# A graph layer's first stage: a third buffer for finished rows and a fifth for the input

## The chip, the cores and the metric

The kernel runs on one core of a Trainium2 chip. The time is that of one launch on the device in microseconds. Three runs gave 759.32, 760.2 and 762.78 us, so the median is 760.2 us. A fourth run was profiled.

## The reference

6250 nodes with 256 features each pass through one layer of a graph network, all in fp32:

```python
xn = layernorm(x)
x = x + gnn(xn, edge_index, weight, attn_l, attn_r) + mix(xn, w_qkv, w_out, b_out)
x = x + moe(layernorm(x), router and expert weights)
```

`gnn` needs two tables per node: `xt = xn @ weight` (256 columns) and the attention scores `xt . attn_l` and `xt . attn_r` of four heads each. For node n it takes the left score of row `src[n]`, the right score and the features of row `dst[n]`, makes a softmax over the four heads and sums the heads with it. `mix` is linear attention: keys and values are products of xn with 512 columns each, normalised per head over 64 columns, and `k^T v` is summed over all nodes. `moe` sends each node to two of six experts of three layers.

## The kernel before, in words

The nodes are laid out as 125 partitions by 50 tiles, `x_t = x.rearrange("(p t) n -> p t n")`. Ten chunks of CH = 5 tiles (CHUNKS) are the unit of transfer. Two tiles make a pair; there are PR = 25 pairs.

**First stage** (what the change touches). For each tile it makes the layer norm xn, its transpose in two parts x_h and x_l (together the exact fp32 value), which stay in SBUF, and the row of both tables, which goes to HBM, since the gathers of the next stage read it there. The engines work on it like this:

- SP (the queue engine) issues all transfers in the order in which its program has them, and a wait or a slow issue holds everything behind it. At the start come chunk 0 in two parts, the graph weights `w_g`, the two attention vectors, chunks 1 to 3, `w_kv` (1 MB into `kv_raw`), then seven small ones. After that, for c = 0 to 9: if chunk c + 4 exists, wait until chunk c is normalised and load chunk c + 4 into the buffer it leaves (XB = 4 buffers `xc`); wait until the rows of chunk c are finished and store them, in three transfers: two for the wide table `xt_tab` (112 and 13 partitions) and one for the score table `al_tab` (125 partitions, 4 floats a row). Behind the loop come the second weights `w_q` and `w_oT`, then the expert weights that the next stage converts (`take`, `put`).
- DVE (VectorE) makes the statistics (L826, L830) of two tiles in each step i, 10 tiles ahead of the products; `finish(c)` (L838, L840) makes a chunk's reciprocal `rs` and `nmr` once ScalarE has taken the root; `lower(i)` (L845) makes x_l of pair i. In steps 12 and 14 it also makes the column means of half of `w_kv` (`centre`, L877, L878). The list STATS_AT says in which step the last statistics of a chunk are made; ScalarE's root follows in that step and `finish` at the start of the next.
- POOL normalises (L519) into a ring of four tiles, and between tiles 29 and 37 subtracts the column means from `w_kv` in four parts (`kv_centre`, L536); between tiles 41 and 48 it makes the lower part of `w_kv` (`kv_lower`, L527). Behind the tiles it waits for all stores and then issues the gathers.
- PE (TensorE) transposes pair i + 1 (L1192) and multiplies pair i by the graph weights (L1198, L1199, L1201) in turn; four PSUM banks hold the results.
- ACT (ScalarE) copies the transposes to x_h (`upper`, L640), the table rows out of PSUM into the ring `xts` (`table`, L647; two chunks long, so that chunk c waits for the store of chunk c - 2), takes the roots (`stdev`, L635) and in steps 17 and 19 casts `w_kv` to its upper part (L667).

**Second stage.** Once the last table row is copied and `w_kv` is ready, PE computes keys and values of each tile and sums `k^T v` (dots, L1221). DVE and ACT normalise them, DVE makes the gathered graph sums (from L923), and at step 2 sets `dotsT` to zero (L979), which lies behind `w_q` and `w_oT` in the space `weight_in` and waits for their load. POOL gathers. The later stages (mixed rows and router, experts) are not touched.

All sizes are fixed by hand: `prep` counts VectorE's linked small steps, and PREP_BO and PREP_W are its values at two points.

## Time and profile before

| what | value |
|---|---|
| median of 3 runs | 760.2 us |
| profiled execution | 756.72 us |
| its span in the profile | 754.7 us |
| mean granted clock of TensorE | 0.945 |
| busy: TensorE, weight loads | 89%, 82% |
| busy: DVE, ACT, POOL | 74%, 58%, 59% |
| moved | 104.68 MB, 139 GB/s |

The span is what the hardware profiler saw from the first instruction to the last, and the execution's own time is 2.0 us longer. The granted clock is the share of 2.4 GHz that TensorE was given: 1.00 is 2.4 GHz and 0.5 is 1.2 GHz. "Idle before" an instruction is the time its engine stood still, with what released it last. A busy share is an average over stages with different limits; only the stage in question tells what a change in it is worth. The page's table of 40 slices has about 19 us in each, so that the first stage is the first four.

### The profile page before, as it was taken

The page shows a single profiled execution, that of the slowest core. Times are in us where ns is not written, and L with a number is a line of the kernel's source. Part 1 is how long each engine was busy: PE and PEld are TensorE (multiplying, and loading weights), DVE is VectorE, ACT ScalarE, POOL GpSimd, SP SyncE. Part 2 cuts the span into 40 slices and gives each one's busy share as a digit, 9 for nine tenths or more (in the row PEclk, how much of TensorE's full clock was granted, in tenths as well). Part 3 has the DMA queues.
Part 4 walks back from the last instruction along what each step waited for, and adds up shares of the span by engine and source line. Part 5 has one row for each costly group of instructions (what it writes and reads, how often), then busy time and mean ns, then how long its engine had stood idle before and what let it go on. Part 6 is the DMA issues. An engine that isn't in the chain of part 4 may idle for free.

```text
span 754.7 us, 15722 instructions
## 1 busy us (share of the span) xinstructions
PE 673.2 (89%) x4705; PEld 621.3 (82%) x4705; DVE 555.3 (74%) x1423; ACT 441.1 (58%) x878; POOL 448.4 (59%) x392
## 2 busy tenths in 40 slices
PE   3878999999999979889885099999999999999993
PEld 2868888888888868777764089999999999999993
DVE  5665569998888876877786357777777777777773
ACT  2546567667776636767763145665665665656651
POOL 3547388877666500325556468888888865455555
PEclk9989999999999999988995579999999999999997
DMA  8785644444444268588734478666546965654443
GB/s 223 164 191 139 162 129 127 125 127 122 128 131 129 62 211 290 170 256 249 222 99 139 130 211 191 122 126 121 113 84 100 173 114 95 98 88 58 50 44 37
DMA packets 90673, 104.68 MB, mean 139 GB/s; under 512 B 27196, under 2 KB 74746, under 8 KB 90594
## 3 DMA queue, kind: packets, MB, share of 16 engines
q1 hardware_dynamic: 58049, 70.98, 33.4%
q0 software_dynamic: 32544, 32.70, 25.0%
q8 instruction: 43, 0.70, 0.4%
q14 instruction: 37, 0.30, 0.1%
HBM read 53.25 MB, written 52.26 MB: 140 GB/s over the span
## 4 chain that ended last, share of the span: by engine, by line
PE 77%; DVE 10%; DMA 3%; ACT 3%; POOL 2%; issue 2%; SPq 1%; POOLq 0%; DVEq 0%; ACTq 0%
PE kv_ps L1357 10%; PE kv_ps L1358 10%; PE kv_ps L1359 10%; PE pt L1349 6%; PE d_ps L1221 6%; PE kv_ps L1198 5%; PE kv_ps L1201 5%; PE kv_ps L1199 5%; PE xt_ps L1349 3%; PE kv_ps L1298 2%; PE pt L1201 2%; PE pt L1198 2%; PE pt L1199 2%; POOL tab L588 1%; PE pt L1289 1%
## 5 line engine op out<-in xcount | busy, mean ns | idle before, releaser
L1357 PE MATMUL kv_ps<-we_h,now_h 128*128 x648 | 193.6, 299 | 3.7 <-DVE now_l L1168 2.2
L1358 PE MATMUL kv_ps<-we_l,now_h 128*128 x648 | 184.4, 285 | 0.0
L1359 PE MATMUL kv_ps<-we_h,now_l 128*128 x648 | 184.3, 284 | 0.0
L1357 PEld LDWEIGHTS kv_ps<-we_h,now_h 128*128 128x128 f32 x648 | 125.1, 193 | 5.2 <-issue 5.2
L1358 PEld LDWEIGHTS kv_ps<-we_l,now_h 128*128 128x128 f32 x648 | 125.4, 194 | 0.0
L1359 PEld LDWEIGHTS kv_ps<-we_h,now_l 128*128 128x128 f32 x648 | 124.9, 193 | 0.0
L1148 DVE TENSOR_TENSOR work<-kv_ps,be 128x256 f32<-128x256 f32 x216 | 81.7, 420 | 52.8 <-PE kv_ps L1359 52.6
L610 POOL DMA_INDIRECT out_x<-work,arena x56 | 87.6, 1564 | 41.9 <-DVE work L1156 26.0
L788 ACT ACTIVATE now_h<-pt 128x512 fp32r<-128x512 f32 x54 | 32.5, 602 | 105.9 <-PE pt L1349 105.9
L556 POOL DMA_INDIRECT alg<-al_tab,src_all x50 | 62.3, 1245 | 39.2 <-issue 25.2
L960 DVE TENSOR_REDUCE ss<-xring 125x16 f32<-125x1040 f32 x50 | 61.7, 1234 | 16.9 <-ACT xring L673 15.9
L559 POOL DMA_INDIRECT arena<-xt_tab,dst_all x50 | 62.0, 1240 | 15.2 <-issue 15.2
L1221 PEld LDWEIGHTS d_ps<-work 125*128 125x128 f32 x400 | 52.0, 191 | 4.8 <-DVE work L974 0.9
L1168 DVE TENSOR_TENSOR now_l<-pt,now_h 128x512 fp32r<-128x512 f32 x54 | 37.4, 692 | 23.5 <-ACT now_h L788 23.5
L588 POOL DMA_INDIRECT tab<-work,pos x14 | 16.8, 1198 | 63.2 <-DVE work L1093 59.5
L773 ACT ACTIVATE staged<-arena 128x256 f32<-128x256 f32 x80 | 43.5, 597 | 18.3 <-DMA arena<-tab 18.3
L1221 PE MATMUL d_ps<-work 125*128 125x128 f32 x400 | 52.5, 275 | 0.7 <-DVE work L974 0.7
L599 POOL DMA_INDIRECT tab<-arena x40 | 40.3, 1007 | 20.4 <-issue 10.9
L1198 PE MATMUL kv_ps<-wkv_h,x_h 128*128 128x512 f32 x120 | 49.7, 414 | 0.6 <-ACT arena L647 0.6
L1349 PE MATMUL pt<-ident,staged 128*128 128x128 f32 x216 | 33.3, 278 | 16.6 <-ACT staged L773 16.6
L588 POOL DMA_INDIRECT tab<-arena,pos x24 | 28.7, 1195 | 32.2 <-DVE arena L1093 25.8
L1199 PE MATMUL kv_ps<-wkv_l,x_h 128*128 128x512 f32 x120 | 47.0, 392 | 0.0
(249 smaller groups left out, 1836.1 us busy)
## 6 DMA issues: line engine op xcount, KB each, us to landing
arena<-tab SPq DMA_DIRECT2D x80, 131.0 KB, 2.9
xring<-in_x SPq DMA_DIRECT2D x26, 224.0 KB
xt_tab<-arena SPq DMA_DIRECT2D x10, 568.8 KB
we_h<-wt_h SPq DMA_DIRECT2D x6, 768.0 KB, 6.0
we_l<-wt_l SPq DMA_DIRECT2D x6, 768.0 KB, 8.8
weight_in<-tab SPq DMA_DIRECT2D x28, 131.0 KB, 2.6
xring<-in_x SPq DMA_DIRECT2D x5, 560.0 KB
out_x<-arena SPq DMA_DIRECT2D x12, 224.0 KB
```

Of the source, the lines that this page charges most:

```text
L556: pool.indirect_dma_start(out=alg[:, b, t % CH, :], out_offset=None, in_=al_tab, in_offset=bass.IndirectOffsetOnAxis(ap=src_all[:, t:t + 1 ...
L559: pool.indirect_dma_start(out=xtg[:, b, t % CH, :], out_offset=None, in_=xt_tab, in_offset=bass.IndirectOffsetOnAxis(ap=dst_all[:, t:t + 1 ...
L610: pool.indirect_dma_start(out=out, out_offset=bass.IndirectOffsetOnAxis(ap=rb[u][:, h, C_TOK:C_TOK + 1].bitcast(I32), axis=0), in_=yw[n % ...
L960: dve.reduce_sum(ss[:, t % 2, :], sq[t % 2], axis=AX.X).then_inc(red_done, 1)
L1148: dve.tensor_tensor(rows[:, h, :], outp[:, h, :], be[layer][:, bass.ds(es[n, h] * F, F)], ALU.add).then_inc(finished, 1)
L1198: pe.matmul(outp, x_h[:, t, c, :], w_h(c), start=c == 0, stop=False)
L1199: pe.matmul(outp, x_h[:, t, c, :], w_l(c), start=False, stop=False)
L1221: last = pe.matmul(d_ps[:, at], vs[t % VB][:, at], ks[t % VB][:, at], start=False, stop=t == T - 1, skip_group_check=True)
L1349: last = pe.transpose(outp[:, h, c, :], rows[:, h, c * 128:(c + 1) * 128], ident[:, :])
L1357: pe.matmul(outp, hi[:, c, :], we_h[:, w], start=c == 0, stop=False)
L1358: pe.matmul(outp, hi[:, c, :], we_l[:, w], start=False, stop=False)
L1359: last = pe.matmul(outp, lo[:, c, :], we_h[:, w], start=False, stop=c == KC - 1)
```

## The change

The ring of finished rows gets a third buffer (XS = 3), placed in `weight_in`, and the input a fifth (XB = 5), placed in `work`. Chunk c then waits for the store of chunk c - 3, and chunk c + 5 is loaded when chunk c is normalised. As the third row buffer lies over part of the space of `w_q` and `w_oT`, their load moves behind the first two expert loads and waits for the last store from that buffer. The column means are made in four pieces, in steps 11 to 14, and POOL waits for one piece only. ScalarE takes a root of one column at the very start, whose result is not used. The whole diff:

```diff
--- before.py
+++ after.py
@@ -23,7 +23,7 @@
 KC = D // 128
 CH = 5
 CHUNKS = T // CH
-XB = 4
+XB, XS = 5, 3
 PR = T // 2
 KB, VB, LAG = 4, 3, 3
 XTW = D + GH
@@ -62,7 +62,7 @@
 ROUTE_STEPS = (0, 1, 9, 15)
 ROUTE = {end - 1: g for g, end in enumerate(ENDS)}
 STATS_AT = {c: max(0, -(-(CH * c - 7) // 2)) for c in range(2, CHUNKS)}
-PREP_EPS, PREP_BO, PREP_W = 1, 13, 18
+PREP_EPS, PREP_BO, PREP_W = 1, 15, 20
 POOL_C = 17
 
 
@@ -129,10 +129,11 @@
 
 
         mix_h, mix_l = wg_h[:, :, 0:D], wg_l[:, :, 0:D]
-        xc = [rows[0:P, b * CH * D:(b + 1) * CH * D].rearrange("p (g n) -> p g n", g=CH)
-              for rows in (xring, gsum_sb) for b in range(2)]
+        xc = [rows[0:P, at:at + CH * D].rearrange("p (g n) -> p g n", g=CH)
+              for rows, at in ((xring, 0), (xring, CH * D), (gsum_sb, 0), (gsum_sb, CH * D), (work, 3 * MI))]
         xn = staged[0:P, 0:4 * D].rearrange("p (g n) -> p g n", g=4)
-        xts = arena[0:P, 0:2 * CH * GW].rearrange("p (g n) -> p g n", g=2 * CH)
+        xts = [rows[0:P, at:at + CH * GW].rearrange("p (g n) -> p g n", g=CH)
+               for rows, at in ((arena, 0), (arena, CH * GW), (weight_in, KC * GW + 3 * D))]
         kv_raw = arena[:, 2 * CH * GW:2 * CH * GW + KC * 2 * MI].rearrange("p (c n) -> p c n", c=KC)
         wg_raw = weight_in[:, 0:KC * GW].rearrange("p (c n) -> p c n", c=KC)
         att_bc = weight_in[:, KC * GW:KC * GW + 2 * D].rearrange("p (s n) -> p s n", s=2)
@@ -142,6 +143,7 @@
         st = sb("st", [P, 2 * CH, 6])
         mv = sb("mv", [P, 2 * CH, 2])
         sd = sb("sd", [P, 2 * CH])
+        first_root = sb("first_root", [128, 1])
         rs = sb("rs", [P, 2 * CH])
         nmr = sb("nmr", [P, 2 * CH])
 
@@ -265,7 +267,7 @@
         mean_done, kv_c, kv_hd, kv_ld = sem("mean_done"), sem("kv_c"), sem("kv_hd"), sem("kv_ld")
         bs_done, ag_done, sd_done, fin_done = sem("bs_done"), sem("ag_done"), sem("sd_done"), sem("fin_done")
         xn_ready, pt_ready, xh_ready, xl_ready = sem("xn_ready"), sem("pt_ready"), sem("xh_ready"), sem("xl_ready")
-        xt_ready, xts_done, xt_out = sem("xt_ready"), sem("xts_done"), [sem(f"xt_out{h}") for h in range(2)]
+        xt_ready, xts_done, xt_out = sem("xt_ready"), sem("xts_done"), [sem(f"xt_out{h}") for h in range(XS)]
 
         k_ready, v_ready, sq_eps = sem("k_ready"), sem("v_ready"), sem("sq_eps")
         sqv_done, red_done, vs_ready, pr_done, sr_done = (sem("sqv_done"), sem("red_done"), sem("vs_ready"),
@@ -409,21 +411,21 @@
                     sp.wait_ge(xn_ready, (c + 1) * CH)
                     load_x(c + XB)
                 sp.wait_ge(xts_done, (c + 1) * CH)
-                rows = slice((c % 2) * CH, (c % 2 + 1) * CH)
                 at = slice(c * CH, (c + 1) * CH)
-                wide(xt_t[:, at, :], xts[:, rows, 0:XTW], xt_out[c % 2])
-                sp.dma_start(al_t[:, at, :], xts[:, rows, XTW:GW]).then_inc(xt_out[c % 2], 16)
-
-
-            sp.wait_ge(wg_ld, 1)
-            sp.wait_ge(prep, PREP_BO)
-            sp.dma_start(wq_sb, chunks(w_q)).then_inc(w3_in, 16)
-            sp.dma_start(woT_sb, chunks(w_oT)).then_inc(w3_in, 16)
+                wide(xt_t[:, at, :], xts[c % XS][:, :, 0:XTW], xt_out[c % XS])
+                sp.dma_start(al_t[:, at, :], xts[c % XS][:, :, XTW:GW]).then_inc(xt_out[c % XS], 16)
+
 
             sp.wait_ge(pt_ready, T)
             take(0)
             sp.wait_ge(kv_ld, 4)
             take(1)
+            sp.wait_ge(wg_ld, 1)
+            sp.wait_ge(prep, PREP_BO)
+            sp.wait_ge(xt_out[2], STORE * len(range(2, CHUNKS, XS)))
+            sp.dma_start(wq_sb, chunks(w_q)).then_inc(w3_in, 16)
+            sp.dma_start(woT_sb, chunks(w_oT)).then_inc(w3_in, 16)
+
             for r in range(ROUNDS):
                 sp.wait_ge(cvl_done, r + 1)
                 put(r)
@@ -532,7 +534,7 @@
                 half, c = part // 2, part % 2
                 cols = slice(half * MI, half * MI + MI)
                 kv_v = kv_raw[:, c, cols].rearrange("p (h n) -> p h n", n=MC)
-                pool.wait_ge(mean_done, half + 1)
+                pool.wait_ge(mean_done, part + 1)
                 pool.tensor_tensor(kv_v, kv_v, kv_mean[:, c, half * MH:half * MH + MH].unsqueeze(2).to_broadcast([128, MH, MC]),
                                    ALU.add).then_inc(kv_c, 1)
 
@@ -545,8 +547,8 @@
             pool.wait_ge(xn_ready, T)
             pool.memset(xring[0:P, 0:4 * MH * SQ].rearrange("p (h n) -> p h n", n=SQ)[:, :, MC:SQ], MC * EPS).then_inc(sq_eps, 1)
 
-            for h in range(2):
-                pool.wait_ge(xt_out[h], STORE * (CHUNKS // 2))
+            for h in range(XS):
+                pool.wait_ge(xt_out[h], STORE * len(range(h, CHUNKS, XS)))
             pool.wait_ge(w2_in, W2)
 
             for t in range(T):
@@ -642,11 +644,13 @@
             def table(t):
 
                 act.wait_ge(xt_ready, t + 1)
-                if t % CH == 0 and t >= 2 * CH:
-                    act.wait_ge(xt_out[t // CH % 2], STORE * (t // CH // 2))
-                act.activation(xts[:, t % (2 * CH), :], banks[t % 4][0:P, 0:GW], ACT.Copy).then_inc(xts_done, 1)
+                c = t // CH
+                if t % CH == 0 and c >= XS:
+                    act.wait_ge(xt_out[c % XS], STORE * (c // XS))
+                act.activation(xts[c % XS][:, t % CH, :], banks[t % 4][0:P, 0:GW], ACT.Copy).then_inc(xts_done, 1)
 
             act.wait_ge(prep, PREP_EPS)
+            act.activation(first_root[:, :], eps_sb[:, :], ACT.Sqrt)
             stdev(0)
             act.wait_ge(wg_c, 1)
             act.activation(wg_h[:, :, :], wg_raw, ACT.Copy).then_inc(wg_hd, 1)
@@ -867,13 +871,13 @@
             stats(range(CH, 2 * CH))
             finish(1)
 
-            def centre(half):
-
-                if half == 0:
+            def centre(part):
+
+                half, c = part // 2, part % 2
+                if part == 0:
                     dve.wait_ge(kv_in, 16)
-                cols = slice(half * MI, half * MI + MI)
-                kv_v = kv_raw[:, :, cols].rearrange("p c (h n) -> p c h n", n=MC)
-                mean_v = kv_mean[:, :, half * MH:half * MH + MH]
+                kv_v = kv_raw[:, c, half * MI:half * MI + MI].rearrange("p (h n) -> p h n", n=MC)
+                mean_v = kv_mean[:, c, half * MH:half * MH + MH]
                 link(dve.reduce_sum(mean_v, kv_v, axis=AX.X))
                 dve.tensor_scalar(mean_v, mean_v, -1.0 / MC, None, ALU.mult).then_inc(mean_done, 1)
 
@@ -903,8 +907,8 @@
                     lower(i)
                 if 2 * i + 11 < T:
                     stats(range(2 * i + 10, 2 * i + 12))
-                if i in (12, 14):
-                    centre((i - 12) // 2)
+                if 11 <= i < 15:
+                    centre(i - 11)
             small()
 
 
```

## Rows read from the trace of the kernel before

**Rows 1.** The page: its first line.

```profile
span 754.7 us, 15722 instructions
```

**Rows 2.** Chain that ended last, first stage: start us, us, engine, what, line.

```profile
30.36 0.43 PE pt L1192 x4
...
32.26 0.43 PE pt L1192 x4
...
54.47 0.83 PE pt L1192 x4
...
57.89 0.40 ACT arena L647
...
80.33 0.47 PE kv_ps L1198
```

**Rows 3.** Timeline of PEld: start, us, engine, line, op, operands [idle before, releaser].

```profile
28.63 0.19 PEld L1198 LDWEIGHTS kv_ps<-wg_h,x_h 128*128 128x128 f32 x1 [0.75 <-DVE x_l L845]
...
38.63 0.19 PEld L1198 LDWEIGHTS kv_ps<-wg_h,x_h 128*128 128x128 f32 x1 [1.58 <-DVE x_l L845]
...
51.46 0.29 PEld L1198 LDWEIGHTS kv_ps<-wg_h,x_h 128*128 128x128 f32 x1 [4.09 <-DVE x_l L845]
...
58.31 0.19 PEld L1198 LDWEIGHTS kv_ps<-wg_h,x_h 128*128 128x128 f32 x1 [0.27 <-DVE x_l L845]
...
67.56 0.19 PEld L1198 LDWEIGHTS kv_ps<-wg_h,x_h 128*128 128x128 f32 x1 [0.84 <-DVE x_l L845]
```

**Rows 4.** Timeline of ACT (ScalarE), first stage.

```profile
7.34 1.28 ACT L635 ACT_TABLE_LOAD   x1 [7.34 <-DVE mv L830]
...
36.99 0.39 ACT L647 ACTIVATE arena<-kv_ps 125x264 f32<-125x264 f32 x1 [2.94 <-DMA al_tab<-arena]
...
51.59 0.39 ACT L647 ACTIVATE arena<-kv_ps 125x264 f32<-125x264 f32 x1 [3.02 <-DMA al_tab<-arena]
...
64.97 0.39 ACT L647 ACTIVATE arena<-kv_ps 125x264 f32<-125x264 f32 x1 [1.24 <-DMA al_tab<-arena]
```

**Rows 5.** Timeline of DVE (VectorE), first stage.

```profile
9.71 0.85 DVE L857 TENSOR_TENSOR work<-weight_in 128x512 f32<-128x512 f32 x1 [0.34 <-DMA weight_in<-in_a_l]
...
47.72 0.43 DVE L826 BATCH_NORM_STATS2 st<-gsum_sb 125x6 f32<-125x256 f32 x1 [1.99 <-DMA gsum_sb<-in_x]
...
48.28 1.19 DVE L877 TENSOR_REDUCE work<-arena 128x16 f32<-128x1024 f32 x1
...
49.80 1.02 DVE L840 SCALAR_TENSOR_TENSOR nmr<-mv,rs 125x5 f32<-125x5 f32 x1
```

**Rows 6.** Timeline of POOL, first stage.

```profile
49.76 1.04 POOL L536 TENSOR_TENSOR arena<-arena,work 128x512 f32<-128x512 f32 x1 [5.30 <-DVE work L878]
```

**Rows 7.** Timeline of the SP queue: start and length of issuing, not of the transfer.

```profile
30.58 3.64 SPq L375 DMA_DIRECT2D gsum_sb<-in_x  x2
...
36.29 5.32 SPq L375 DMA_DIRECT2D gsum_sb<-in_x  x2
41.65 0.87 SPq L375 DMA_DIRECT2D xt_tab<-arena  x2
...
43.51 5.59 SPq L375 DMA_DIRECT2D xring<-in_x  x2
49.15 0.87 SPq L375 DMA_DIRECT2D xt_tab<-arena  x2
...
51.31 4.85 SPq L375 DMA_DIRECT2D xring<-in_x  x2
58.30 0.85 SPq L375 DMA_DIRECT2D xt_tab<-arena  x2
```

**Rows 8.** Windows: stretch, length, busy us by engine, granted clock, DMA share, GB/s.

```profile
48.00:54.00 6.00, 2.53 (x11) 2.54 (x12) 5.72 (x18) 1.57 (x4) 4.12 (x6) 0.73 0.82 155
```

**Rows 9.** Timeline of DVE (VectorE), start of the second stage.

```profile
93.16 0.48 DVE L979 MEMSET weight_in<- 128x512 f32 x1
...
106.12 0.18 DVE L923 TENSOR_TENSOR al<-alg,arena 125x20 f32<-125x20 f32 x1 [4.07 <-DMA arena<-xt_tab,dst_all]
```

## The prediction

> **What bounds the kernel now.** I read the page first, then TensorE's idle time, then what ended each idle stretch on the other engines. The profiled execution took 756.7 us: a span of 754.7 us [rows 1] and 2.0 us around it. The change touches the first stage, which ends when the first key product starts at 80.33 [rows 2]. From there TensorE is busy in every slice of the table until the next stage, so what counts is by how much that start moves.
>
> Inside the stage, a pair of tiles costs TensorE 1.9 us at full clock (transposes 30.36 to 32.26, [rows 2]). Twenty-five pairs are 47.6 us, yet the stage takes 80. The idle time of the weight loads tells where the rest is [rows 3]. A gap of 0.75 us stands once per chunk: x_l waits for the chunk's root and reciprocal. It is there where nothing is late, and the change leaves it. Three gaps are of another kind: 1.58 us at 38.63, 4.09 us at 51.46 and 0.84 us at 67.56.
>
> ScalarE names the first cause [rows 4]: it stands 2.94, 3.02 and 1.24 us in front of the first tile of chunks 3, 5 and 7, until the store of the chunk two before has landed and its half of the ring is free. VectorE names the second [rows 5]: at 47.72 it had waited 1.99 us for chunk 7 of the input, then came the mean of half the key/value weights (1.19 us), and then nmr took 1.02 us. POOL's centring op ran 49.76 to 50.80, just over that nmr [rows 6]. The queue engine names the third [rows 7]: issuing one chunk's load took it 3.64, 5.32, 5.59 and 4.85 us, and the stores stand behind it. A turn of load and store lasted 7.2 us (36.29 to 43.51) and 7.8 us (43.51 to 51.31), more than the 4.8 us that 2.5 pairs need.
>
> After the 4.09 us gap TensorE ran at its lower level. The window 48 to 54 us has a granted clock of 0.73, a mix of 2.4 and 1.2 GHz [rows 8], and transposes took 0.83 us instead of 0.43 [rows 2].
>
> **The change part by part, on TensorE's path.**
>
> Third buffer for finished rows: chunk c now waits for the store of c-3. Chunk 3 waits for chunk 0, stored long before. Of the 1.58 us at 38.63, 0.25 us is only the offset that a weight load has from its matmul, so **1.3 us** goes. The bounds are 0.8 (if an ordinary 0.75 us gap comes there) and 1.3.
>
> Gap at 51.46: I take it down to an ordinary gap, 4.09 - 0.75 = **3.3 us**. It needs all three of its causes gone, since they stand in a row. (a) Chunk 7 of the input is loaded one turn earlier, in the place that chunk 6 had: issue at 30.58 instead of 36.29 [rows 7]. It landed 11.4 us after the start of its issue; 30.58 + 11.4 = 42.0, and VectorE would want it near 44. (b) Column means in four pieces: each about 0.6 us (half of 1.19) plus a small scaling of under 0.2 us, in four steps instead of 1.2 us in two. Two of the four stand in steps in which VectorE waits for ScalarE's root anyway; the other two may add 0.2 us each, covered by the x_l order. Two more instructions of 0.2 us in all; I count 0, bounds 0 and 0.4. (c) The collision with POOL: the first mean comes one step earlier, so POOL, which had idled 5.30 us for it [rows 6], centres before the nmr instead of over it.
>
> nmr took 1.02 us with one POOL op over it; four POOL ops still follow, so one or two may hit again, under 1.0 us each: bounds 0 and 2, and I take 0. The Trainium skill (SBUF — State Buffer, "SBUF: two separate sides") says that a VectorE op with two SBUF inputs and a GpSimd op lock each other out of a shared port for a whole instruction. By it every meeting of the two costs up to the rest of the other's op, which speaks against spreading the centring over more of the stage; the trace agrees at 49.80.
>
> Low clock: the pair from 54.47 to 57.89 took 3.4 us against 1.9, the pair before it (51.47 to 54.47) 3.0 against 1.5. That is **2.9 us**, which goes if the gap in front of it goes. It stays whole if it does not; the 1.58 us gap was followed by no such fall, the 4.09 us gap was.
>
> Gap at 58.31: only 0.27 us [rows 3], since the slow clock covered an ordinary gap of 0.75. At full clock it is back: **-0.5 us**.
>
> Gap at 67.56, behind chunk 7's wait of 1.24 us [rows 4]. Chunk 7 now needs the store of chunk 4. The load of chunk 9 moves to the turn at 43.51 and holds the queue 5.6 us, so that store is again issued at 49.15 [rows 7]. A store took between 6.6 us from its issue to its landing (58.30 to 64.93, the one that ended the third wait) and 9.9 us (41.65 to 51.55, the second), so it lands at 55.8 to 59.1. By the terms so far chunk 7 comes to it at 63.7 - 7.0 = 56.7. So the wait is 0 to 2.4 us against 1.24: I count **0** for this gap, bounds +0.8 and -1.5.
>
> Fifth input buffer: the queue issues the same descriptors. Load 4 goes out ahead of the key/value weights, which land later by its share of the engines, some 3 us by the shortest load issue there [rows 7]; they are read first at 48.28 [rows 5], so 0. If that cover were gone it would be those 3 us.
>
> Early root table: its 1.28 us load moves off the first root [rows 4]. But the next link, VectorE's first product at 9.71, waits for the attention vector's transfer [rows 5], while the root began right behind its table load, at 8.6. Worth **0**; without that wait it would be 1.28.
>
> Second weights later: the two loads now stand behind two expert loads and one more wait. They are moved past no store. They land perhaps 1.5 us later relative to the stage's start. Before, they were there when VectorE asked (93.16, no idle before it), and it later idled 4.07 us for the gathered rows at 106.12 [rows 9]. A wait of up to 4 us at step 2 is swallowed there: **0**. POOL's gathers start when the last store has landed, as before; that idle stretch of 4.07 us did not reach TensorE, which was busy throughout, but how much longer it could be no row shows. I bound a later last store by 0 and 2 us.
>
> Sum: 1.3 + 3.3 + 2.9 - 0.5 = **7.0 us**. 756.7 becomes 749.7. The median of the runs shown is 760.2, 3.5 us above the profiled one, which I take as the same offset: **753.2 us**. A measurement of this kernel tells apart about 0.5%, 3.8 us.
>
> **The rivals.**
>
> *Fuller gain.* No wait is left on the stores, and no gap beyond 0.75 us stays. Then 0.8 of the gap at 67.56 goes too, and the 0.5 at 58.31 stays covered: 8.3 us, 751.9 us. Against: the stores still queue behind the loads.
>
> *The queue stays the bound.* The loads come too late for VectorE although issued earlier, since the transfers themselves are what is slow: with 0.82 of the engines busy only 155 GB/s moved [rows 8]. The small store of 16-byte rows that closes each chunk is the suspect. The Trainium skill (DMA: Bandwidth & Descriptors, "Why a DMA increments its semaphore by 16 and not by 1") says that a copy uses the largest count of engines up to 16 that divides both partition counts. For 125 partitions that would be 5, so they would back up while others idle, and a third buffer would not help. By rows: the 1.99 us for the input stay in the big gap, which is then 4.09 - 1.19 for the mean and nearly 1 for nmr, so 2.0 us, and the clock falls after it. Of 7.0 remain 7.0 - 1.3 - 2.9 = 2.8 us: 757.4 us, no change that can be told. For it: the queue engine is without a pause from 36 to 56 us [rows 7]. Against: one whole turn more of lead.
>
> *Slower: the store of chunk 4 behind the load of chunk 9.* If with five chunks in flight each load holds the queue 5.6 us from load 6 on (two turns 2 to 3 us longer each), that store is issued at about 55 and lands at 64 to 65. ScalarE then stands 8 us before chunk 7 with the cast of the weights and x_h behind it, TensorE idles about as long, and the clock falls once more, 2.9 us. 8.0 + 2.9 - 7.0 = 3.9 us slower, 764.1 us. It decides once the store lands later than about 60.8 (56.7 + 7.0 - 2.9). For it: issues grew from 3.64 to 5.59 as the loads went on. Against: the total of bytes is the same, and after load 9 nothing is queued.
>
> **How the numbers follow.** My forecast has a chance of 0.60, with a range of its own of 750.5 to 756; the fuller gain 0.17, the queue bound 0.16, the slower case 0.07. The range, 748.5 to 758.5, takes in the fuller gain less 3.4 us (two more ordinary gaps, 1.5, and about 2 us that the runs shown spread) and the queue bound plus 1. Left out are the slower case and tails. Faster by over 0.5% (below 756.4): the forecast and the fuller gain, 0.77, and a little of the queue bound, together 0.78. Within 0.5%: 0.15. Slower: 0.07.
>
> **What would show it.** The first key product starts near 73.3. No wait of ScalarE on a store before chunks 3 and 5; at most 2.4 us before chunk 7. No wait for chunk 7 of the input. Granted clock 1.00 from 20 us to the stage's end. The queue engine still without a pause, its last load issued near 43.5. The stages behind keep their length. Wrong would be: a gap over 2 us with a clock under 0.8 after it; a wait of VectorE in front of the memset at step 2 that reaches TensorE; or a start near 73 while the total does not follow.

## The result, and the profile after

Four runs of the changed kernel took 751.75 to 754.05 us, median 752.92 us, and four of the kernel before 760.54 us. The ratio is 0.9914 with a 95% interval of 0.989 to 0.9938: 6.5 us faster by the ratio, 7.6 by the medians. The forecast was 753.2 us.

The profile says something less comfortable. Its execution took 754.05 us, only 2.7 us less than the profiled one of before (756.72 us). The page's first line and its row of the granted clock, and the start of the second stage in the chain:

```profile
span 751.9 us, 15726 instructions
...
PEclk9999999999999999989995579999999999999997
```

```profile
66.96 0.83 PE pt L1196 x4
...
77.52 0.47 PE kv_ps L1202
```

The second stage starts at 77.52 us, against 80.33 before [rows 2]: 2.8 us earlier, which is the whole difference of the two spans (754.7 - 751.9). Forecast was 73.3. The transposes at 66.96 took 0.83 us, so the lower clock is still there, in another place. The gaps of TensorE's weight loads, to be read against [rows 3]:

```profile
39.08 0.19 PEld L1202 LDWEIGHTS kv_ps<-wg_h,x_h 128*128 128x128 f32 x1 [0.75 <-DVE x_l L849]
...
45.58 0.19 PEld L1202 LDWEIGHTS kv_ps<-wg_h,x_h 128*128 128x128 f32 x1 [0.75 <-DVE x_l L849]
...
50.49 0.19 PEld L1202 LDWEIGHTS kv_ps<-wg_h,x_h 128*128 128x128 f32 x1 [0.75 <-DVE x_l L849]
...
55.88 0.19 PEld L1202 LDWEIGHTS kv_ps<-wg_h,x_h 128*128 128x128 f32 x1 [1.56 <-DVE x_l L849]
...
64.38 0.19 PEld L1202 LDWEIGHTS kv_ps<-wg_h,x_h 128*128 128x128 f32 x1 [3.67 <-DVE x_l L849]
```

The gaps of 1.58 us and of 4.09 us are gone, and what is left of both places is the ordinary 0.75. But there are two that this profile of before has not, 1.56 us at 55.88 and 3.67 us at 64.38. ScalarE's timeline names their cause (against [rows 4]):

```profile
46.11 0.39 ACT L650 ACTIVATE weight_in<-kv_ps 125x264 f32<-125x264 f32 x1 [1.60 <-DMA al_tab<-weight_in]
...
53.96 0.67 ACT L650 ACTIVATE arena<-kv_ps 125x264 f32<-125x264 f32 x2 [3.35 <-DMA al_tab<-arena]
...
61.79 0.39 ACT L650 ACTIVATE arena<-kv_ps 125x264 f32<-125x264 f32 x1 [4.09 <-DMA al_tab<-arena]
```

These are the first tiles of chunks 5, 6 and 7, which wait for the stores of chunks 2, 3 and 4. The wait of 1.60 us reaches TensorE only as a gap of 0.31 us; the other two do as shown. The queue engine (against [rows 7]):

```profile
38.31 5.22 SPq L377 DMA_DIRECT2D gsum_sb<-in_x  x2
43.57 0.87 SPq L377 DMA_DIRECT2D xt_tab<-arena  x2
...
45.51 5.36 SPq L377 DMA_DIRECT2D work<-in_x  x2
50.91 0.87 SPq L377 DMA_DIRECT2D xt_tab<-arena  x2
...
53.10 6.10 SPq L377 DMA_DIRECT2D xt_tab<-weight_in  x2
```

Loads 8 and 9 are issued at 38.31 and 45.51 and hold the queue for 5.22 and 5.36 us. The store of chunk 3 stands between them, issued at 43.57 and landed at 53.9, 10.3 us later; that of chunk 4, at 50.91, landed at 61.7, 10.8 us later. The next line of the queue is the wide store of chunk 5; no load stands between it and the stores of chunk 4, and its issue took 6.10 us all the same. A turn of load and store lasted 7.2 and 7.6 us (38.31 to 45.51 to 53.10), as before the change (7.2 and 7.8 [rows 7]). The clock, by windows (against [rows 8]):

```profile
48.00:54.00 6.00, 5.48 (x45) 5.25 (x45) 4.62 (x18) 1.97 (x6) 5.48 (x9) 1.00 0.86 160
66.00:72.00 6.00, 6.00 (x43) 5.94 (x42) 2.45 (x5) 4.28 (x11) 5.46 (x7) 0.81 0.70 123
```

Granted clock 1.00 where 0.73 stood before, and 0.81 later, behind the gap of 3.67 us. One more wait, which the prediction does not name: VectorE waited 0.70 us at 56.86 for chunk 9 of the input.

### The profile page after: what moved, and what is told of

Same layout as the page of the kernel before. It is cut to its first block, busy times and chain, and to the rows that moved or that the text cites. A ratio compares the mean times of both kernels' runs of the same rounds, so it can differ in the third digit from the quotient of the medians.

```text
span 751.9 us, 15726 instructions
## 1 busy us (share of the span) xinstructions
PE 670.3 (89%) x4705; PEld 619.2 (82%) x4705; DVE 554.2 (74%) x1427; ACT 442.1 (59%) x879; POOL 448.3 (60%) x392
## 4 chain that ended last, share of the span: by engine, by line
PE 77%; DVE 10%; ACT 3%; DMA 3%; POOL 3%; issue 2%; SPq 1%; POOLq 0%; DVEq 0%; ACTq 0%
PE kv_ps L1361 10%; PE kv_ps L1362 10%; PE kv_ps L1363 10%; PE pt L1353 6%; PE d_ps L1225 6%; PE kv_ps L1202 5%; PE kv_ps L1205 5%; PE kv_ps L1203 5%; PE xt_ps L1353 3%; PE kv_ps L1302 2%; PE pt L1202 2%; PE pt L1205 2%; PE pt L1203 2%; POOL tab L590 1%; DMA al_tab<-arena 1%
## 5 line engine op out<-in xcount | busy, mean ns | idle before, releaser
L777 ACT ACTIVATE staged<-arena 128x256 f32<-128x256 f32 x80 | 43.5, 598 | 18.3 <-DMA arena<-tab 18.3
L1202 PE MATMUL kv_ps<-wkv_h,x_h 128*128 128x512 f32 x120 | 49.7, 414 | 0.6 <-ACT arena L650 0.6
```

Source lines behind the costliest of these rows:

```text
L1202: pe.matmul(outp, x_h[:, t, c, :], w_h(c), start=c == 0, stop=False)
```

## The experiments

The twelve runs were made in three groups, each on a chip of its own (the record numbers them 4, 8 and 6). The kernel before takes 784.6, 782.1 and 786.1 us there, against 760.5 us in the result above, for which no number is recorded. Ratios are to the kernel before on the same chip. "Start" is where the first weight load of the second stage stands in the profile; it is compared best within one chip, and even there the third chunk's first product starts up to 1.3 us apart from profile to profile. The theories of the first group (chip 4): A, my prediction's, that the waits for stores and for the input each cost TensorE and the buffers take them away; B, that the queue of transfers is the bound, and buffers only move the wait; C, for the third row buffer, that the stores were the whole cause. From the second group on the letters name two reasons for the long issues: A their bytes, B the small store in front of them.

| kernel | chip | ratio, 95% interval | start, us |
|---|---|---|---|
| before, second profile | 8 | 1.0005 (0.9985 to 1.0025) | 84.47 |
| third row buffer alone | 4 | 0.9948 (0.9925 to 0.9972) | 81.52 |
| fifth input buffer alone | 4 | 0.9973 (0.9953 to 0.9993) | 82.23 |
| mean in pieces and early root alone | 4 | 1.0007 (0.9987 to 1.0027) | 85.32 |
| changed kernel again | 4 | 0.9904 (0.9882 to 0.9925) | 77.16 |
| changed, without early root | 8 | 0.9931 (0.9907 to 0.9955) | 77.14 |
| changed, mean in halves | 6 | 0.9932 (0.9909 to 0.9955) | 78.76 |
| before, small store in 112 + 13 | 8 | 0.9957 (0.9934 to 0.998) | 80.13 |
| changed, small store in 112 + 13 | 8 | 0.9852 (0.9814 to 0.989) | 71.40 |
| changed, small store in 115 + 10 | 6 | 0.9915 (0.9887 to 0.9943) | 79.76 |
| 112 + 13, four inputs | 6 | 0.9855 (0.9802 to 0.9908) | 72.86 |
| 112 + 13, mean in halves | 6 | 0.9837 (0.9808 to 0.9867) | 72.09 |

### Was the first profile of before typical?

> The kernel before, unchanged, for a second profile. Its first profiled execution took 3.8 us less than its median. If the first stage is what varies between executions, this profile has the stage ending later than 80.3 us, near 84, and the time before and the changed kernel's first profile are not to be subtracted from each other. If the rest of the kernel varies, the stage ends at 80 to 81 us again. Ratio 1.

The stage ended at 84.47 us, 4.1 us later than in the first profile. Weight loads and ScalarE of this second profile of the kernel before:

```profile
52.41 0.29 PEld L1198 LDWEIGHTS kv_ps<-wg_h,x_h 128*128 128x128 f32 x1 [3.34 <-DVE x_l L845]
...
71.37 0.19 PEld L1198 LDWEIGHTS kv_ps<-wg_h,x_h 128*128 128x128 f32 x1 [3.51 <-DVE x_l L845]
...
84.47 0.19 PEld L1198 LDWEIGHTS kv_ps<-wkv_h,x_h 128*128 128x128 f32 x1 [0.76 <-issue]
```

```profile
52.57 0.39 ACT L647 ACTIVATE arena<-kv_ps 125x264 f32<-125x264 f32 x1 [3.07 <-DMA al_tab<-arena]
...
68.79 0.39 ACT L647 ACTIVATE arena<-kv_ps 125x264 f32<-125x264 f32 x1 [3.92 <-DMA al_tab<-arena]
```

The mid-stage gap is there, a little shorter (3.34 us). What differs is chunk 7: its wait for a store lasts 3.92 us where it lasted 1.24 [rows 4], and the gap behind it is 3.51 us. So the first profile had caught a short wait, and one of 3 to 4 us before chunk 7 belongs to the kernel before as well. That the short wait is chance and not the other chip is an inference: the changed kernel's stage took the same on the chips (77.52, 77.16, and 77.14 without the early root), but no second profile of before was taken on the result's chip.

> The changed kernel once more, for a second profile and for the difference on this chip. Theory A (new wait before chunks 6 and 7 for stores that stand behind the loads, as in its first profile: 3.4 and 4.1 us): the same two waits within 1 us each, and the first stage ends at 77 to 78 us in the profile; 6 to 8 us faster than before by the medians. If the new waits are chance, the stage ends near 73 to 74 us.

```profile
58.88 0.19 PEld L1202 LDWEIGHTS kv_ps<-wg_h,x_h 128*128 128x128 f32 x1 [1.68 <-DVE x_l L849]
...
64.00 0.19 PEld L1202 LDWEIGHTS kv_ps<-wg_h,x_h 128*128 128x128 f32 x1 [3.19 <-DVE x_l L849]
...
77.16 0.19 PEld L1202 LDWEIGHTS kv_ps<-wkv_h,x_h 128*128 128x128 f32 x1 [0.75 <-issue]
```

```profile
56.98 0.43 DVE L830 BATCH_NORM_STATS2 st<-work 125x6 f32<-125x256 f32 x1 [1.43 <-DMA work<-in_x]
```

ScalarE's waits before chunks 6 and 7 were 1.81 and 3.60 us, the start 77.16. Chunk 7's wait came back within 1 us, chunk 6's did not (3.35 us in the first profile), and it left no gap: the 1.68 us at 58.88 stand behind VectorE's wait of 1.43 us for chunk 9 of the input, the chunk in the new fifth buffer. Between the second profiles the stage ends 7.3 us earlier (84.47 to 77.16); they come from two chips, but on chip 8 alone, from before to the changed kernel without the early root, it is 84.47 to 77.14, of which 1.0 us was there when the third chunk began. The time agrees: the ratio of 0.9904 is 7.5 us of 784.6 (by the medians 6.7). Read against the second profile of before, the change has taken away the gap of mid-stage and the low clock behind it, and has left the gap that chunk 7's store causes (3.51 us at 71.37 there, 3.19 and 3.67 us in the two profiles of the changed kernel).

### Each part alone

Third row buffer (with the later second weights), the rest as before:

```diff
-XB = 4
+XB, XS = 4, 3
...
-                if t % CH == 0 and t >= 2 * CH:
-                    act.wait_ge(xt_out[t // CH % 2], STORE * (t // CH // 2))
+                c = t // CH
+                if t % CH == 0 and c >= XS:
+                    act.wait_ge(xt_out[c % XS], STORE * (c // XS))
```

> The kernel before with the third buffer for finished rows alone, and the later second weights that it needs. Theory A (each wait on a store costs TensorE, and the gap of 4 us in mid-stage has three causes in a row): the wait of ScalarE before chunk 3 goes (1.3 us), the wait of VectorE for chunk 7 of the input, the mean in two halves and the meeting with POOL stay, so the big gap and the low clock behind it stay: 758 to 760 us, 1 to 2 us faster than before. Theory B (the queue of transfers is the bound, buffers only move the wait): within 1 us of before. Theory C (the stores were the whole cause): 5 us or more faster, and no gap over 1 us on TensorE.

4 us faster, between theories A and C. From 20 us on ScalarE waited for no store. The input became the wait:

```profile
49.19 0.43 DVE L828 BATCH_NORM_STATS2 st<-gsum_sb 125x6 f32<-125x256 f32 x1 [4.45 <-DMA gsum_sb<-in_x]
```

```profile
52.93 0.29 PEld L1200 LDWEIGHTS kv_ps<-wg_h,x_h 128*128 128x128 f32 x1 [6.09 <-DVE x_l L847]
```

VectorE stood 4.45 us for chunk 7 of the input and TensorE 6.09 us behind it, the largest gap of all profiles, again with the low clock after it (granted 0.77 and 0.66 in the windows 48 to 54 and 54 to 60 us).

Fifth input buffer alone:

```diff
-XB = 4
+XB = 5
...
-              for rows in (xring, gsum_sb) for b in range(2)]
+              for rows in (xring, gsum_sb) for b in range(2)] + [
+                  work[0:P, 3 * MI:3 * MI + CH * D].rearrange("p (g n) -> p g n", g=CH)]
```

> The kernel before with the fifth input buffer alone; rows still have two buffers. Theory A: VectorE no longer waits for chunk 7 of the input, but ScalarE waits for the stores of chunks 1 to 5 as before or longer, since each load stands ahead of a store: gap in mid-stage shorter by up to 2 us, 0 to 3 us faster than before. Theory B: a load that goes out earlier delays the store behind it, so 0 to 3 us slower. Theory C: within 1 us of before.

2 us faster, as theory A allowed. It is the mirror image: no wait for an input chunk after the first, but ScalarE waited for five stores, 1.98, 3.66, 2.45, 4.54 and 3.53 us, of which these are the fourth and fifth:

```profile
54.19 0.39 ACT L648 ACTIVATE arena<-kv_ps 125x264 f32<-125x264 f32 x1 [4.54 <-DMA al_tab<-arena]
...
62.15 0.67 ACT L648 ACTIVATE arena<-kv_ps 125x264 f32<-125x264 f32 x2 [3.53 <-DMA al_tab<-arena]
```

The stores of chunks 3 and 4 were issued at 43.82 and 51.87 us, 1.2 and 1.4 us later than in the second profile of before (42.61 and 50.43, on another chip). I read it so: a load stands ahead of each store, and with two row buffers its earlier turn costs ScalarE part of what it saves VectorE.

Mean in pieces and early root alone:

```diff
+            act.activation(first_root[:, :], eps_sb[:, :], ACT.Sqrt)
             stdev(0)
...
-                if i in (12, 14):
-                    centre((i - 12) // 2)
+                if 11 <= i < 15:
+                    centre(i - 11)
```

The centring itself and POOL's waits for it are those of the change.

> The kernel before with the column means in four pieces and the early root table alone. By my prediction both are worth 0 without the buffers: the big gap is then ended by the wait for the store (51.6) as before, within 1 us of before. By what the trace of the changed kernel shows, the first chunk runs 0.6 us earlier with the early root, so 0.6 us faster is the other expectation. If the meeting of nmr and POOL and the long mean were what ended the big gap: 2 to 5 us faster, with the clock at 1.00 after 48 us.

No difference in time. The gap in mid-stage fell to 2.41 us (at 50.78) and the clock stayed at 1.00 from 48 to 60 us, and nmr took 0.17 us, so the long mean and the meeting with POOL did have a part in the gap. The stage did not end earlier for it, since the wait for the store before chunk 7 (4.03 us) gave a gap of 3.61 us at 71.08. The parts alone are worth 4.1, 2.1 and -0.5 us, 5.7 together; the whole is worth 7.5. With these intervals, some 2 us wide to each side, the sum doesn't show that they need each other; the profiles point to it, in that each buffer alone leaves the other's wait.

Without the early root, all else as changed (the diff above without its first line):

> The changed kernel without the early root table. By my prediction (hidden behind the attention vector's transfer): within 0.3 us of the changed kernel, and the start of the third chunk's keys at 23.4 in the profile. By what the trace showed (0.6 us earlier in the first chunk, since TensorE's clock rose earlier): that start is 0.6 us later, 24.0, and the time 0.5 us longer, if nothing later absorbs it.

The ratio is 0.9931 against 0.9904, with intervals that overlap, and the stage ends at 77.14 against 77.16. The third chunk's graph products (the expectation calls them keys) start at 23.50 us without it and at 23.44 and 24.35 us with it. No effect shown. The granted clock was 1.00 from 60 to 72 us in this profile, though a gap of 2.85 us stood at 64.42. With the fifth input alone it fell to 0.72 between 42 and 46 us behind a gap of 2.31 us. So which gap costs the clock can't be told from its length alone. This profile also holds the test of the later second weights:

```profile
92.85 0.48 DVE L981 MEMSET weight_in<- 128x512 f32 x1 [2.89 <-DMA weight_in<-in_w_oT]
...
103.05 0.18 DVE L925 TENSOR_TENSOR al<-alg,arena 125x20 f32<-125x20 f32 x1 [2.43 <-DMA arena<-xt_tab,dst_all]
```

VectorE waited 2.89 us for the second weights and then 2.43 us for the gathered rows, where it had waited 4.07 us before [rows 9]. TensorE was busy throughout from 80 to 110 us. VectorE's last step of this kind (L925; L923 in before) started 186.8 us after the start of the second stage, as in both profiles of before and in the changed kernel with the mean in halves, where the wait for the second weights was 3.40 us. The wait was swallowed where the prediction had put it.

Mean in halves, all else as changed (the centring of the kernel before, with its waits and counts):

> The changed kernel with the column means in two halves again, all else as changed. If the pieces matter although the transfers bound the stage: 1 to 3 us slower than the changed kernel (ratio to before 0.993 to 0.994 instead of 0.990), with a gap of 1.5 us or more near tile 26. If the later waits for stores absorb it: the gap is there, but the stage ends at 77 us all the same, ratio 0.990.

```profile
45.37 1.02 DVE L844 SCALAR_TENSOR_TENSOR nmr<-mv,rs 125x5 f32<-125x5 f32 x1
```

```profile
47.03 0.19 PEld L1202 LDWEIGHTS kv_ps<-wg_h,x_h 128*128 128x128 f32 x1 [1.75 <-DVE x_l L849]
...
52.95 0.19 PEld L1202 LDWEIGHTS kv_ps<-wg_h,x_h 128*128 128x128 f32 x1 [1.99 <-DVE x_l L849]
...
78.76 0.19 PEld L1202 LDWEIGHTS kv_ps<-wkv_h,x_h 128*128 128x128 f32 x1 [0.76 <-issue]
```

Two gaps of 1.75 and 1.99 us stand where the changed kernel has 0.75, and the stage ends 1.6 us later than in its second profile, on another chip. The ratio, 0.9932, would be 2 us slower than 0.9904, but the intervals overlap. The nmr in front of each gap took 1.02 us, with a POOL centring op of 1.04 us started 0.04 or 0.05 us before it (45.33 and 51.24). With the mean in pieces it takes 0.17 us: the meeting with POOL accounts for 0.85 us (1.02 - 0.17) of the 1.0 and 1.2 us by which these gaps exceed 0.75.

### Why the queue is slow

The traces of before and after keep every packet that the transfer engines moved, and the packets of 16 bytes in this stage are all from the small store, 625 for each chunk. They show where a load's long issue ends:

| kernel | small store's packets start, us | load issued behind it: issue ends, us |
|---|---|---|
| before | 26.0 to 27.4 | 27.3 |
| before | 33.0 to 34.3 | 34.2 |
| before | 40.1 to 41.6 | 41.6 |
| before | 47.6 to 49.1 | 49.1 |
| before | 54.8 to 56.4 | 56.2 |
| after | 27.6 to 29.3 | 29.6 |
| after | 34.9 to 36.3 | 36.3 |
| after | 42.2 to 43.5 | 43.5 |
| after | 49.7 to 51.2 | 50.9 |

Each time the issue ended within 0.4 us of the start of the last small packet. Such a coincidence can have the load waiting for the small store, or both waiting for something before them; the next runs decide.

Each chunk closes with a store of 125 partitions with rows of four floats. I split it as the wide store is split:

```diff
-                sp.dma_start(al_t[:, at, :], xts[c % XS][:, :, XTW:GW]).then_inc(xt_out[c % XS], 16)
+                wide(al_t[:, at, :], xts[c % XS][:, :, XTW:GW], xt_out[c % XS])
...
-        STORE = 16 * 3
+        STORE = 16 * 4
```

> The changed kernel, but the small store of each chunk (16-byte rows) is sent in two transfers of 112 and 13 partitions, like the wide one, not in one of 125. Theory B (that store crowds a few transfer engines, and the next load waits for them): each load's issue falls from 5.5 us to 3 us or less, the waits of ScalarE before chunks 6 and 7 go, the stage ends at 73 to 74 us, 3 to 4 us faster than the changed kernel. Theory A (the queue is long because of its bytes): issues stay over 5 us, within 1 us of the changed kernel, or slower by the ten more issues of 0.4 us.

The time falls to 0.9852 of before, 11.6 us less, and the stage ends earlier than theory B had asked. The queue engine of this version:

```profile
36.19 1.08 SPq L377 DMA_DIRECT2D gsum_sb<-in_x  x2
...
39.53 1.90 SPq L377 DMA_DIRECT2D al_tab<-arena  x2
41.47 1.01 SPq L377 DMA_DIRECT2D work<-in_x  x2
```

A load's issue takes 1.0 us where it took 5.2 and 5.4, the small store's 1.90 instead of 1.0, and the queue pauses between. The stage in windows and in weight loads:

```profile
20.00:60.00 40.00, 36.32 (x291) 34.45 (x290) 31.74 (x112) 26.90 (x63) 24.09 (x41) 1.00 0.95 207
```

```profile
45.60 0.19 PEld L1202 LDWEIGHTS kv_ps<-wg_h,x_h 128*128 128x128 f32 x1 [0.75 <-DVE x_l L849]
...
56.99 0.19 PEld L1202 LDWEIGHTS kv_ps<-wg_h,x_h 128*128 128x128 f32 x1 [0.75 <-DVE x_l L849]
...
71.40 0.19 PEld L1202 LDWEIGHTS kv_ps<-wkv_h,x_h 128*128 128x128 f32 x1 [0.75 <-issue]
```

The transfer engines moved 207 GB/s between 20 and 60 us, 187 in the changed kernel without the early root on the same chip. ScalarE waited for no store, VectorE for no input chunk after the first. From 20 us on no gap is over the ordinary 0.75 us except one of 0.96 us, and the stage ends at 71.40 us, 5.7 us before the changed kernel without the early root (77.14). Their times don't touch: 766.26 to 770.74 us against 775.17 to 778.34.

> The kernel before with only the small store of each chunk sent in two transfers of 112 and 13 partitions. Theory B: the waits for stores that stand in the profile of before (2.9, 2.1, 3.0, 1.2 us) shrink to under 1 us and so does the wait for chunk 7 of the input; 5 to 8 us faster than before, as much as the change itself. Theory A: within 1 us of before.

In the kernel before the same edit gave 0.9957, 3.4 us: less than theory B wanted. Load issues fell to between 0.8 and 2.1 us, but with two row buffers ScalarE still waited 3.71, 1.08, 2.57 and 2.70 us. Its stage ended at 80.13 us, 4.3 us before the second profile of before. The stores that these four waits ended on (chunks 1, 3, 4 and 5) landed 6.8 to 10.4 us after their issue, and one spare buffer does not cover that.

Control, two transfers as well, but of 115 and 10 partitions:

```diff
-                sp.dma_start(al_t[:, at, :], xts[c % XS][:, :, XTW:GW]).then_inc(xt_out[c % XS], 16)
+                for part in SMALL:
+                    sp.dma_start(al_t[part, at, :], xts[c % XS][part, :, XTW:GW]).then_inc(xt_out[c % XS], 16)
...
-        STORE = 16 * 3
+        STORE = 16 * 4
+        SMALL = (slice(0, 115), slice(115, P))
```

> Control for the kernel with the small store in 112 and 13 partitions: the same two transfers, but of 115 and 10 partitions. If what helped was over how many transfer engines the small rows are spread (115 has only the divisor 5 up to 16), load issues stay over 5 us, the waits before chunks 6 and 7 stay, the stage ends at 76 to 78 us, ratio to before 0.990. If what helped was two smaller transfers in place of one, the stage ends at 71 to 72 us and the ratio is 0.985.

```profile
45.88 0.87 SPq L378 DMA_DIRECT2D xt_tab<-arena  x2
46.79 5.78 SPq L418 DMA_DIRECT2D al_tab<-arena  x2
52.61 0.77 SPq L378 DMA_DIRECT2D work<-in_x  x2
```

```profile
55.94 0.67 ACT L652 ACTIVATE arena<-kv_ps 125x264 f32<-125x264 f32 x2 [5.40 <-DMA al_tab<-arena]
...
64.45 0.39 ACT L652 ACTIVATE arena<-kv_ps 125x264 f32<-125x264 f32 x1 [3.80 <-DMA al_tab<-arena]
```

Ratio 0.9915, that of the changed kernel. Two details of the expectation failed. The loads' issues became short (0.77 us): the pair of small transfers now took the block instead, 5.78 us. And the stage ended at 79.76 us, later than the 76 to 78 expected. ScalarE's waits are back, 5.40 and 3.80 us. So it is not that there are two transfers: it is how the partitions divide. The Trainium skill (DMA: Bandwidth & Descriptors, "Why a DMA increments its semaphore by 16 and not by 1") says that a copy is spread over the largest number of engines up to 16 that divides both sides' outer dimension. Worked out from it, 125 and 115 partitions give 5, 112 and 13 give 16 and 13, and 10 give 10. The runs agree with the rule; the number of engines itself stands in no trace here. The packets in flight point the same way. Of those of 16 bytes in the first 90 us at most 10 or 11 were under way at once in each profile with one small store of 125 partitions, 14 with 115 + 10, and 18 to 21 with 112 + 13.

Two parts of the change once more, where the small store is split in 112 + 13. Four inputs instead of five:

> The changed kernel with the small store in 112 and 13 partitions, but with four input buffers. If the fifth buffer was only needed because loads were held by the small store: within 1 us of the version with five, stage ends at 71 to 72 us. If chunk 7 of the input still comes too late (2 us or more of VectorE waiting, as with three row buffers alone, where it was 4.5 us): 2 to 5 us slower than with five, and a gap of over 2 us on TensorE.

```profile
33.44 0.43 DVE L830 BATCH_NORM_STATS2 st<-xring 125x6 f32<-125x256 f32 x1 [1.65 <-DMA xring<-in_x]
...
44.67 0.43 DVE L830 BATCH_NORM_STATS2 st<-gsum_sb 125x6 f32<-125x256 f32 x1 [0.65 <-DMA gsum_sb<-in_x]
```

VectorE waits 1.65 us for an input chunk in the first half and 0.65 us for chunk 7, where it was 4.45 us with the blocked queue. The stage ends at 72.86, 1.5 us later than with five (on another chip) and 0.9 us past the expected 71 to 72. The ratio, 0.9855, is that of five inputs (0.9852), but its interval is 4 us wide to each side. So most of what the fifth buffer covered was the blocked queue; whether the 1.5 us of the profile are left the times can't tell.

Mean in halves:

> The changed kernel with the small store in 112 and 13 partitions, but with the column means in two halves (steps 12 and 14) again. My prediction's step, on a path where no transfer is late any more: the half mean of 1.2 us stands in front of the reciprocal and nmr in steps 12 and 14, and POOL waits for it; gaps of TensorE near tiles 26 and 30 grow from 0.75 to 1.5 to 3 us, 1.5 to 4 us slower than with pieces. If ScalarE's root covers it, within 1 us.

```profile
45.81 0.19 PEld L1202 LDWEIGHTS kv_ps<-wg_h,x_h 128*128 128x128 f32 x1 [1.75 <-DVE x_l L849]
...
51.17 0.19 PEld L1202 LDWEIGHTS kv_ps<-wg_h,x_h 128*128 128x128 f32 x1 [1.54 <-DVE x_l L849]
...
72.09 0.19 PEld L1202 LDWEIGHTS kv_ps<-wkv_h,x_h 128*128 128x128 f32 x1 [0.76 <-issue]
```

The gaps near tiles 26 and 30 are 1.75 and 1.54 us instead of 0.75, 1.8 us in all, and the stage ends 0.7 us later, though its third chunk had started 0.8 us earlier (22.67 against 23.46). The ratio (0.9837) shows no loss. The pieces' gain is in the profile, and under 2 us.

This run and the one with the mean in halves before it differ in the small store alone and ran on one chip. That makes them the cleanest pair: 777.25 to 783.44 us (eight runs) with 125 partitions, 772.01 to 774.70 (four runs) with 112 and 13, and 78.76 against 72.09 us for the start of the second stage (1.2 us of the 6.7 was there when the third chunk began). The 115 + 10 version on the same chip took 777.08 to 781.44 us.

## Why the prediction was right, and where it was not

The total was right to 0.3 us, and that is luck in part: the forecast held two errors of about 4.5 us each that cancelled. The profiled execution came 4.4 us above my sum (754.05 against 749.7), and the offset that I added to it, +3.5 us, was -1.1.

*Third row buffer, 1.3 us.* Right: the gap of 1.58 us is gone, and no wait for a store stands before chunk 3. But I had said the same of chunk 5, and there ScalarE waited 1.60 us (1.96 us without the early root, none in the second profile); TensorE felt 0.31 us of it.

*Gap of 4.09 us, taken down to 0.75.* Right in size and in its causes. The gap at 45.58 us is 0.75. The runs with parts alone showed each cause: with the input late it is 6.09 us (third buffer alone), with mean and nmr in the way 1.75 and 1.99 us (halves), and with the mean in pieces alone, input and stores as before, 2.41 us. In the changed kernel each piece of the mean took 0.65 us, and both nmr in that stretch (44.77 and 49.68) took 0.17 us: no meeting with POOL's centring, as taken.

*Low clock, 2.9 us.* Right at its old place, but it came back behind the new gap of 3.67 us: 0.81 in the window 66 to 72 us, transposes at 0.83 us. By the windows TensorE lost 3.4 us of full clock before (6 us at 0.73 and 6 us at 0.70, from 48 to 60) and 1.7 us after (0.91 and 0.81, from 60 to 72), so about half of the term was given back. Against the second profile of before it holds in full: there the clock was 0.77 and 0.66 from 48 to 60 us and again 0.74 from 72 to 78.

*Gap at 67.56, "I count 0, bounds +0.8 and -1.5".* This is the step that failed. I took a store to land 6.6 to 9.9 us after its issue and let the wait be at most 2.4 us. They took 10.3 and 10.8 us, chunk 7 waited 4.09 us, and chunk 6, which I had not costed, 3.35 us. For chunk 7 the parts can be told: its store was issued at 50.91 and not at 49.15, it took 0.9 us more to land than my upper bound, and ScalarE came to it at 57.7, 1.0 us later than I had taken.

The gap was 3.67 us against 0.84 in the first profile of before, so this term was -2.8 us and not 0, with the 1.7 us of low clock behind it. Against the second profile of before (3.51 us) it is nearly 0: the third buffer did not shorten this wait, and the short one of the first profile was my baseline. It is the store of chunk 4 behind the load of chunk 9, the mechanism of the rival that I gave 0.07, at the right place, at about half of its 8 us and without its slower total. The queue's turn stayed at 7.2 and 7.6 us with more buffers while the chunks came sooner, so a wait stayed where I had counted none. The third row buffer alone shows it from the other side: its stores went out at nearly the same times (42.85 and 50.64 us), but TensorE had stood 6.09 us for the input, the chunks came late, and no store was waited for.

*The offset of 3.5 us between the profiled execution and the median.* I took it for the same in both kernels. It was not: the changed kernel's profiled execution took 1.1 us more than its median. The second profile of before ended its stage 4.1 us later than the first, and the start of 73.3 us that I forecast was 4.2 us too early (77.52). Against the second profile of before the stage gained 7.3 us, which is near my 7.0; against the first, 2.8. That the first profile's shortness lay in its first stage is inferred from chip 8's profile.

*The queue as bound, 0.16.* It was the bound: loads held it 5.2 and 5.4 us, a wide store 6.1. But chunk 7 of the input, for which its price kept the wait, came in time, so the price (757.4) was wrong. VectorE waited for chunk 9 instead, 0.70 and 1.43 us. Its suspect, the small store, was the right one, which the versions with 112 + 13 and 115 + 10 partitions show.

*The rest at 0.* Early root, later second weights and mean pieces' own cost: 0 within what can be measured. The wait for the second weights was seen (0.37 us in the changed kernel's first profile, up to 3.40 us in others) and did not reach TensorE between 80 and 110 us.

The version that beats both kernels is the changed one with its small store in 112 and 13 partitions: 0.9852 of before, against 0.9904 for the change itself. The ends of these two intervals (0.989 and 0.9882), from two chips, overlap slightly; the pairs on one chip, with times that don't touch, do not leave it in doubt.

## What to carry to other kernels

Before adding buffers, look at how long the issue of a transfer takes. A load that needs 5 us to be issued need not be slow itself: here it stood behind a store of 10 KB over 125 partitions, and dividing that store otherwise made the load's issue 1 us. And if one queue carries both loads and stores and is full, a buffer for the one leaves the wait for the other; here the fifth input alone left up to 4.54 us on a store, the third row buffer alone 4.45 us on the input. Last, take a second profile of the kernel before: a sum against a single execution carries that execution's luck.

## What was not expected

The transfer of rows of 16 bytes, 10 KB in all, decided what 1.3 MB per chunk cost: changed only in how its partitions were divided, it brought the loads' issue from 5.4 to 1.0 us.

The three chips of the experiments were 22 to 26 us slower with the same kernel than the result's, and apart from the 4.1 us of the first stage told above hardly any of it lay in the stages studied. From the start of the second stage to the first product of the experts the kernel before took 353.6 us in its first profile (80.3 to 433.9) and 353.2 us in its second (84.5 to 437.7). The experts' products took 310.3 us in the first (to 744.2) and 332.8 us in the second (to 770.5). Between profiles of the experiments that last stretch varied (329.0 us in the version with 112 + 13, 335.1 us in the changed kernel), which is why spans of single profiles are not compared above. Why it is slower there stays open.
